# A vision tower with routed experts: the token step rearranged on all engines

## The chip, the cores and the metric

The kernel runs on one core of a Trainium2 chip. The metric is the device time of one execution in microseconds (us). A core has five engines that run side by side, each with its own queue that it works through in order, and that meet only at semaphores: TensorE (PE in the profile: matmuls and turnings, that is transposes), VectorE (DVE), ScalarE (ACT), GpSimd (POOL) and SyncE (SP), which issues transfers. DMA engines move the data. TensorE writes into eight banks of PSUM, from which DVE and ScalarE copy into SBUF.

## The reference, cut to what matters

128 images of 64x64x3 make 16 patches each, 2048 tokens of 768 values. All is float32.

```python
h = patches @ W.T + b                                  # 768 -> 192
q, k, v = split(layernorm(h) @ W_attn + b_attn)        # 12 heads of 16, rotary on q and k
h = h + causal_attention(q, k, v) @ W_proj + b_proj    # 16 tokens of an image among themselves
x = layernorm(h)                                       # (h - mean) / sqrt(var + eps)
t = x / sqrt(mean(x * x) + eps) * norm_scale           # rmsnorm
g = t @ gate_w.T + gate_b                              # 16 experts
top 4, weights = softmax of the four values
y = sum over the four: weight * (swiglu(t @ mlp1_w + mlp1_b) @ mlp2_w + mlp2_b)
out = h + x + y
```

The mean of x * x after a layernorm is var / (var + eps), so both roots follow from the same variance; the kernel before computes the second from the values.

## The kernel before, in words

There are two phases. In the **token phase** 16 tiles of 128 tokens (8 images) go through seven stages, and the queues of all engines are written out by hand (`unrolled(STAGES, TILES, step)`): in step n every engine does stage 0 of tile n, stage 1 of tile n - 1, up to stage 6 of tile n - 6, in an order of its own, which its `step` function gives. So there are 22 steps, of which 6 to 15 have all stages. Stage 0 is the embedding (L410) and the first norm (DVE, with its root on POOL); 1 the turning of the normed tile (`xnT`), the product to q and k (L432) and to v (L436), the rotary products; 2 the turnings of q and k (L416), `spread_keys` (ScalarE, six copies), the scores (L448), their maximum and, as the kernel was, the exponential `prob` (L680); 3 the sums and inverses (`prob_sum` L815, `prob_inverse_own` L824), `p_pair` on POOL (L1106), its turning on DVE (`turn_probs`), `spread_probs` (ScalarE, four copies), the values (L476), and their copy `yT`; 4 the projection (L455), the second norm with two roots and the residual `base`; 5 the turning of the token (`tT`), the gate, the four largest; 6 weights, rank of each token within its expert, row numbers `row_i` (L940), the bias of the experts (L466), and the **scatters**: POOL sends each tile's packet (192 values, 16 weights, a token number) to four rows of `routed_rows` by four indirect DMAs (L1093).

Semaphores tell of each result; a `wait` is a wait on one. Two buffers each of `packet` and `row_i` go round. SP meanwhile loads one expert's weights in every step (seven DMAs) and the next x.

Between the phases, DVE computes `fill_i` (L964) once the last tile is counted; SP, ScalarE and POOL write 8, 6 and 2 regions' padding rows (L310), and a table of 79 tiles is made. In the **expert phase** each of 79 tiles of 128 rows is loaded (L384), turned (L562), copied to `rT` by ScalarE (L617, the copy helper's line, in `r_step` L712), multiplied with its expert's weights (L580, L584), gated (L719), multiplied again (L592) and added to the output by an indirect DMA (L1149).

The order of three queues in a step, cut to what the change moves:

```python
# PE: embed(0), turn xn(1), turn q, k(2), project(4), rank(6), turn token(5), qk_product(1),
#     turn_weights(6), gate(5), scores(2), values(3), experts_bias(6), v_product(1)
# ACT: packet(6), xnT(1), qT(2), spread_keys(2), tT(5), spread_probs(3), combT(6), square(4),
#      yT(3), prob(2), top_e(5), v_sb(1)
# POOL: p_pair(3), root(0), root(4), four scatters(6), second root(4), residual(4)
```

Of the kernel before, what the change touches and what calls it, by code (L numbers as in the profile page):

```python
# [8 lines left out]
ALU = mybir.AluOpType  # L9
# [7 lines left out]
P = 128  # L17
# [13 lines left out]
EPS = 1e-5  # L31
LIMIT, ALPHA = 7.0, 1.702
# [14 lines left out]
STAGES = 7  # L47
R_STAGES = 3
# [48 lines left out]
def build(nc, x, consts, w_tok, b_tok, w_qkv, b_qkv, w_proj, nscale, w_gate, b_gate,  # L97
          w1, b1, w2, b2, out):
    routed = nc.dram_tensor("routed_rows", (SPARE + P, ROW), F32, kind="Internal").ap()
    with ExitStack() as ctx:  # L100
# [28 lines left out]
        nscale_bc = sb("nscale_bc", [P, DIM])  # L129
        power = sb("power", [P, 1])  # L130
# [27 lines left out]
        stats2, mv2, ve2, rstd2 = sb("stats2", [P, 6]), sb("mv2", [P, 2]), sb("ve2", [P, 1]), sb("rstd2", [P, 1])  # L158
        x2, x2sq = sb("x2", [P, DIM]), sb("x2sq", [P, DIM])
        ssq, msq, rms = sb("ssq", [P, 1]), sb("msq", [P, 1]), sb("rms", [P, 1])  # L160
        t_row = [sb(f"t_row{i}", [P, DIM]) for i in range(2)]
        packet = [sb(f"packet{i}", [P, ROW]) for i in range(2)]
        tT = sb("tT", [HALF + 1, 2, P])
        top_v, top_i, top_f = sb("top_v", [P, 8]), sb("top_i", [P, 8], U32), sb("top_f", [P, TOPK])
# [5 lines left out]
        comb = sb("comb", [P, EXPERTS])  # L170
# [4 lines left out]
        row_f = sb("row_f", [P, TOPK])  # L175
# [31 lines left out]
        ps_e, ps_cT = banks[0][:, 0:DIM], banks[0][0:EXPERTS, 256:256 + P]  # L207
        ps_qk = banks[1][:, 0:2 * DIM]

        def turned(b, a, rows=HALF):  # L210
# [5 lines left out]
        ps_qT, ps_b = turned(3, 0), banks[3][:, 256:256 + DIM]  # L216
        ps_kT, ps_g = turned(4, 0), banks[4][:, 256:256 + EXPERTS]
        ps_v, ps_p = banks[5][:, 0:DIM], banks[5][:, 256:256 + DIM]
        ps_xT, ps_tT = turned(6, 0), turned(6, 256)
        ps_s = banks[7][:, 0:HEADS * GROUP]  # L220
        ps_tab = banks[3][0:1, 0:3 * SLOTS]
        ps_b1 = banks[4][:, 0:2 * ICH * EXPERTS]
# [9 lines left out]
        b1_turned = sem("b1_turned")  # L232
# [6 lines left out]
                 "ve2_ready rstd2_ready x2_ready base_ready ssq_ready msq_ready rms_ready t_row_ready t_turned packed "  # L239
                 "tT_ready gated top_v_ready top_i_ready top_f_ready top_d_ready top_e_ready einv_ready top_w_ready "  # L240
                 "onehot_ready onehot_w_ready comb_ready weights_ready token_ready chosen_ready ranked comb_turned "
                 "combT_ready b2_done base_full place_ready onehot_r_ready row_f_ready row_i_ready "
                 "chosen_before_ready").split()
        s = {n: sem(n) for n in names}
        scattered = [sem("scattered0"), sem("scattered1")]
# [17 lines left out]
        def rows_out(t, buf):  # L263

            return (t - buf) * 8 * TOPK
# [50 lines left out]
        def _(sp):  # L316
# [58 lines left out]
            for buf in range(2):  # L375
                sp.wait_ge(scattered[buf], 16 * TOPK * TILES // 2)
# [831 lines left out]
```

## Time and profile before

| | us |
|---|---|
| median of 3 runs (545.75 to 549.13) | 546.63 |
| the profiled execution: its time | 546.29 |
| its span | 544.6 |
| TensorE busy | 454.4 (83%) |
| DVE busy | 304.7 (56%) |
| ScalarE busy | 310.6 (57%) |
| POOL busy | 254.6 (47%) |

The rows further down come from one profiled execution. Times are from the start of the span. "Busy" is the time in which an engine had an instruction of its own in work; waits and DMA-issuing are not in it, and the ends of matmuls are modelled. In a timeline a row says when an instruction (or several of a line, merged) started, how long it took, and in brackets how long the engine had been idle before it and whose signal ended that: "remote" is a releaser that the profile can't name, "issue" a stretch in which the engine waited for nothing that it shows.

### The profile page before, as it was taken

Reading aid. Unit: us, or ns where it says so; the run is one execution under the profiler, and the core shown is the slowest. Engines: PE = TensorE matmul, PEld = TensorE weight load, DVE = VectorE, ACT = ScalarE, POOL = GpSimd, SP = SyncE. Lnnn points to the kernel's source line nnn. Section 1 sums busy time; section 2 is a strip of 40 time slices with the busy share of each in tenths; the row PEclk is TensorE's granted clock in tenths of the full one; section 3 lists DMA queues with packets and bytes.
Section 4 is the critical chain, followed back from the end, with each engine's and each line's share of the span. In section 5 each row is a group of like instructions: output and inputs, shape, how many; then the busy total and the mean of one; then the engine's idle time right before and its main releaser. Section 6 shows DMA issues by size and latency. Waiting matters only on the chain.

```text
span 544.6 us, 14479 instructions
## 1 busy us (share of the span) xinstructions
PE 454.4 (83%) x3865; PEld 394.8 (72%) x3866; DVE 304.7 (56%) x964; ACT 310.6 (57%) x832; POOL 254.6 (47%) x303
## 2 busy tenths in 40 slices
PE   3888988878887765129999999999999999999960
PEld 2666776557665544028999999999999999999950
DVE  0367978887787656304555555555555555555530
ACT  1248656665667631036667666667666667666630
POOL 1114576667766557502444444444444444444332
PEclk9989989999898655559999999999999999999995
DMA  8955455554541112431334333333333333433221
GB/s 220 267 145 164 138 158 165 172 162 149 158 121 40 40 42 85 135 104 37 58 63 63 54 53 61 61 61 59 57 52 61 61 61 54 62 51 62 41 24 21
DMA packets 41901, 49.55 MB, mean 91 GB/s; under 512 B 6387, under 2 KB 33251, under 8 KB 41860
## 3 DMA queue, kind: packets, MB, share of 16 engines
q1 hardware_dynamic: 26452, 33.48, 22.7%
q0 software_dynamic: 14544, 14.94, 16.9%
q10 hardware_dynamic: 864, 0.65, 0.4%
q8 instruction: 18, 0.29, 0.2%
q14 instruction: 23, 0.19, 0.1%
HBM read 30.82 MB, written 18.23 MB: 90 GB/s over the span
## 4 chain that ended last, share of the span: by engine, by line
PE 48%; DMA 12%; DVE 11%; issue 10%; ACT 5%; POOL 4%; SPq 4%; another core or an unknown queue 4%; POOLq 1%; DVEq 0%; ACTq 0%
PE bank L580 16%; PE bank L592 11%; PE bank L584 10%; DMA out_rows<-x_sb,wtok_sb 6%; PE bank L562 4%; DMA out_rows<-x_sb,wproj_sb 3%; PE bank L410 2%; POOL routed_rows L1093 2%; ACT p_spread L617 2%; ACT k_spread L635 2%; DMA out_rows<-x_sb,pT 1%; SPq L309 1%; DMA x_sb<-patches 1%; SPq L310 1%
## 5 line engine op out<-in xcount | busy, mean ns | idle before, releaser
L1149 POOL DMA_INDIRECT out_rows<-x_sb,wtok_sb x50 | 78.6, 1573 | 130.2 <-DMA out_rows<-x_sb,wtok_sb 73.8
L580 PE MATMUL bank<-rT,w_now 128*128 128x128 f32 x948 | 120.1, 277 | 0.9 <-ACT rT L617 0.9
L580 PEld LDWEIGHTS bank<-rT,w_now 128*128 128x128 f32 x948 | 117.2, 193 | 1.7 <-ACT rT L617 1.7
L1038 DVE TENSOR_TENSOR v_sb<-bank,w_now 128x384 f32<-128x384 f32 x79 | 44.1, 558 | 117.2 <-PE bank L584 97.3
L617 ACT ACTIVATE w_now<-w_sb 128x1158 f32 x79 | 92.5, 1171 | 6.9 <-issue 1.7
L592 PE MATMUL bank<-w_sb,p_spread 128*128 x474 | 90.3, 327 | 1.1 <-DVE p_spread L1057 1.1
L617 ACT ACTIVATE rT<-bank 128x256 f32<-128x256 f32 x79 | 30.3, 383 | 89.8 <-PE bank L562 69.0
L592 PEld LDWEIGHTS bank<-w_sb,p_spread 128*128 128x128 f32 x474 | 75.2, 190 | 1.5 <-issue 1.4
L584 PE MATMUL bank<-rT,w_now 64*128 64x128 f32 x948 | 74.9, 291 | 0.0
L1093 POOL DMA_INDIRECT routed_rows<-packet,row_i x64 | 63.3, 989 | 24.2 <-issue 22.3
L719 ACT ACTIVATE k_spread<-bank,w_now 128x128 f32<-128x128 f32 x237 | 69.3, 370 | 1.9 <-PE bank L584 1.9
L584 PEld LDWEIGHTS bank<-rT,w_now 64*128 64x128 f32 x948 | 59.6, 189 | 9.6 <-issue 0.2
L1050 DVE TENSOR_SCALAR x_sb<-bank,row_w 128x192 f32<-128x192 f32 x79 | 33.0, 418 | 29.7 <-PE bank L592 28.5
L1149 POOL DMA_INDIRECT out_rows<-x_sb,wproj_sb x20 | 31.3, 1564 | 38.2 <-DMA out_rows<-x_sb,wproj_sb 20.7
L410 PE MATMUL bank<-wtok_sb,x_sb 128*128 128x192 f32 x192 | 40.2, 367 | 9.9 <-DMA wtok_sb<-w_tok 6.4
L410 PEld LDWEIGHTS bank<-wtok_sb,x_sb 128*128 128x128 f32 x192 | 37.8, 220 | 10.0 <-DMA wtok_sb<-w_tok 6.1
L1057 DVE SCALAR_TENSOR_TENSOR p_spread<-k_spread,v_sb 128x384 f32<-128x384 f32 x79 | 43.3, 549 | 0.8 <-ACT k_spread L719 0.8
L1043 DVE TENSOR_SCALAR v_sb<-v_sb 128x384 f32<-128x384 f32 x79 | 34.9, 442 | 2.7
L635 ACT ACTIVATE k_spread<-bank,cst 96x256 f32<-96x256 f32 x96 | 36.4, 481 | 0.0
L617 ACT ACTIVATE p_spread<-pT 32x384 f32<-32x384 f32 x64 | 33.1, 518 | 0.7
L562 PE MATMUL bank<-cst,wtok_sb 128*128 128x128 f32 x100 | 22.3, 306 | 13.4 <-DMA wtok_sb<-routed_rows 13.4
L617 ACT ACTIVATE yT<-bank 128x384 f32<-128x384 f32 x16 | 7.8, 490 | 41.2 <-remote 37.9
(150 smaller groups left out, 634.6 us busy)
## 6 DMA issues: line engine op xcount, KB each, us to landing
x_sb<-patches SPq DMA_DIRECT2D x16, 384.0 KB, 3.4
w_sb<-w SPq DMA_DIRECT2D x32, 192.0 KB
wtok_sb<-routed_rows SPq DMA_DIRECT2D x50, 106.0 KB
w_sb<-w SPq DMA_DIRECT2D x16, 288.0 KB
w_sb<-w SPq DMA_DIRECT2D x64, 48.0 KB
wproj_sb<-routed_rows SPq DMA_DIRECT2D x20, 106.0 KB
out_rows<-h SPq DMA_DIRECT2D x16, 96.0 KB
routed_rows<-packet,row_i POOLq DMA_INDIRECT x64
```

The lines of the kernel that those rows point to most:

```text
L410: last = mm(ps_e, x_sb[buf][:, c, :], wtok_sb[:, c, :], start=(c == 0), stop=(c == PCH - 1))
L562: last = turn(ps_rT[buf % 2][:, c, :], rows[buf][:, a:a + P], ident)
L580: mm(dst[:, c * P:(c + 1) * P], w[:, a:a + P], t[:, part, :], start=(c == 0), stop=False)
L584: last = mm(dst[:, c * P:(c + 1) * P], w[k:k + half, REST + c * P:REST + (c + 1) * P], t[k:k + half, 1 - part, :], start=False, stop=(c == ...
L592: last = mm(ps_yo[buf % 2], act_sb[buf % 2][:, c, :], w2_sb[:, bass.ds(expert, 1), c, :].rearrange("p a f -> p (a f)"), start=(c == 0), st ...
L617: return nc.scalar.activation(dst, src, ACT.Copy)
L635: last = nc.scalar.activation(k_spread[:, :, :, h], ps_kT.rearrange("p c (j i k) -> p c j i k", j=PAIRS, i=2), ACT.Copy, scale=const("head ...
L719: last = nc.scalar.activation(gate_act[b][:, a:a + P], ps_glu[b][:, a:a + P], ACT.Silu, bias=w1_now[b][:, GLU_B + c:GLU_B + c + 1], scale= ...
L1038: V.tensor_tensor(lin[b].rearrange("p (c t) -> p c t", c=ICH), ps_lin[b][:, 0:INNER].rearrange("p (c t) -> p c t", c=ICH), w1_now[b][:, LI ...
L1057: V.scalar_tensor_tensor(act_sb[b].rearrange("p c t -> p (c t)"), gate_act[b], SILU_LIMIT, lin[b], ALU.min, ALU.mult).then_inc(r["act_read ...
L1093: G.indirect_dma_start(out=routed, out_offset=bass.IndirectOffsetOnAxis(ap=row_i[buf][:, k:k + 1].bitcast(U32), axis=0), in_=packet[buf][: ...
L1149: G.indirect_dma_start(out=out, out_offset=bass.IndirectOffsetOnAxis(ap=rows[b][:, ID_AT:ID_AT + 1].bitcast(U32), axis=0), in_=y_out[b % N ...
```

## The change

It rearranges the token phase; the expert phase is as it was but for one copy.

- TensorE: the turnings of xn, q, k and the token come first in a step, then the q and k product, rank, the weights' turning, the projection, the embedding, gate, scores, bias, v product, and the values last.
- ScalarE: `prob` moves from the end of a tile's stage 2 to the start of its stage 3, `yT` from stage 3 to stage 4, the copy `v_sb` from the end of stage 1 to stage 2. The packet's copy and the square are gone; the residual (h1 scaled by `gain` plus `shift`) is new here.
- DVE: `norm2` writes the token straight into the packet, with the product of both roots as its scale. `norm3`, `top_float`, `fill_packet`'s copy of the weights and `place_whole` are gone; `gain` and `shift` are new; the order is another.
- POOL: one operation makes the two roots of a tile from its variance; the second root and the residual sum are gone. A tile's scatters are issued one step later, the first ahead of `p_pair`, two behind it, the fourth behind the roots; the last two tiles' are issued in the last step.
- The norm's gain no longer multiplies the token: at the start four small matmuls and three DVE operations turn it into a column and scale the gate's weights, and in the expert phase `rT` is scaled by it, in two ScalarE copies of 128 columns instead of one of 256.
- Four packets go round instead of two, and `ps_b`, `ps_g` and `ps_cT` change banks.

```diff
+T_EPS, T_SCALE = EPS * EPS / (1.0 + EPS), (1.0 + EPS) ** -0.5
+PACKETS = 4
+        ps_e, ps_b = banks[0][:, 0:DIM], banks[0][:, 256:256 + DIM]
+        ps_qT, ps_g = turned(3, 0), banks[3][:, 256:256 + EXPERTS]
+        ps_s, ps_cT = banks[7][:, 0:HEADS * GROUP], banks[7][0:EXPERTS, 384:384 + P]
...
         @block.tensor                      # step, new order
+                if tile(1) is not None:
+                    bank_free(("xnT_ready", seen(1, 1)), ("tT_ready", seen(5, 1)))
+                    turn_halves(tile(1), ps_xT, xn, "xn_ready", "xn_turned")
+                ...                        # q, k (2)
+                if tile(5) is not None:
+                    turn_halves(tile(5), ps_tT, packet[tile(5) % PACKETS], "t_row_ready", "t_turned")
+                ...                        # qk_product(1), rank(6), turn_weights(6), project(4), embed(0)
                 if isinstance(tile(0), int) and tile(0) == 0:
...
+                    for c in range(2):
+                        a = c * (DIM - P)
+                        mm(ps_ns[:, c:c + 1], ns_line[:, a:a + P], ident[0:1, 0:1], start=True, stop=True)
+                    for c in range(2):
+                        last = mm(ps_ns[0:HALF, 2 + c:3 + c], ns_line[:, c * HALF:(c + 1) * HALF], ident[0:1, 0:1],
+                                  start=True, stop=True)
+                    last.then_inc(ns_turned, 1)
+                    pe.wait_ge(setup_dve, 5)
+                ...                        # gate(5), scores(2), experts_bias(6), v_product(1)
+                if tile(3) is not None:
+                    bank_free(("yT_ready", seen(3, 1)), ("place_ready", seen(6)))
+                    values(tile(3), (n - 3) % 2)
...
         @block.scalar                      # step, new order
+                # prob(3), xnT(1), qT(2), v_sb(2), tT(5), yT(4), spread_keys(2), combT(6), spread_probs(3)
+                if tile(4) is not None:
+                    act.wait_ge(s["shift_ready"], t + 1)
+                    nc.scalar.activation(h0[:, t, :], h1[:], ACT.Identity, bias=shift[:], scale=gain[:]
+                                         ).then_inc(s["base_ready"], 1)
+                # top_e(5)
...
-                    copy(rT[b0 % 2][:], ps_rT[b0 % 2]).then_inc(r["rT_ready"], 1)
+                    for c in range(2):
+                        last = nc.scalar.activation(rT[b0 % 2][:, c, :], ps_rT[b0 % 2][:, c, :], ACT.Copy,
+                                                    scale=ns_row[:, c:c + 1])
+                    last.then_inc(r["rT_ready"], 1)
...
         @block.vector
+            V.tensor_scalar(ns_row[:], ps_ns[:, 0:2], T_SCALE, None, ALU.mult).then_inc(setup_dve, 1)
+            V.tensor_scalar(ns_gate[:], ps_ns[0:HALF, 2:4], T_SCALE, None, ALU.mult).then_inc(setup_dve, 1)
+            V.tensor_tensor(gate_w, gate_w, ns_gate[:].unsqueeze(2).to_broadcast([HALF, 2, EXPERTS]), ALU.mult
+                            ).then_inc(setup_dve, 1)
...
             def norm2(t):
+                packed = packet[t % PACKETS]
+                dve.wait_ge(s["roots_ready"], t + 1)
+                wait(dve, scattered[t % PACKETS], rows_out(t, t % PACKETS))
+                V.tensor_scalar(packed[:, 0:DIM], h1[:], mv2[:, 0:1], roots[:, 0:1], ALU.subtract, ALU.mult
+                                ).then_inc(s["t_row_ready"], 1)
+                V.tensor_scalar(gain[:], roots[:, 1:2], 1.0, None, ALU.add).then_inc(s["gain_ready"], 1)
+                V.scalar_tensor_tensor(shift[:], mv2[:, 0:1], -1.0, roots[:, 1:2], ALU.mult, ALU.mult
+                                       ).then_inc(s["shift_ready"], 1)
...
             def place_sum(t):
+                if t >= 2:
+                    dve.wait_ge(scattered[(t - 2) % PACKETS], rows_out(t + PACKETS - 2, (t - 2) % PACKETS))
+                    V.tensor_reduce(row_i[buf][:], onehot_r[:], AX_X, ALU.add).then_inc(s["row_i_ready"], 1)
...
+                # DVE's new order: mark_experts(6), choose_experts(6), prob_sum(3), top_weights(6),
+                #  prob_inverse(3), prob_inverse_own(3), weigh_experts(6), combine(6), note_token(6),
+                #  [fill_i], rope_products(1), turn_probs(3), attn_add(4), attn_stats(4), place_all(6),
+                #  attn_aggr(4), rope_add(1), place_chosen(6), place_sum(6), norm2(4), embed_add(0),
+                #  embed_stats(0), top_max(5), embed_aggr(0), top_index(5), score_first(2),
+                #  score_second(2), score_max(2), norm(0), score_minus_max(2), add_bias(6)
...
         @block.gpsimd
+            def attn_roots(t):
+                pool.wait_ge(s["mv2_ready"], t + 1)
+                alone(pool)
+                G.tensor_tensor(ve2[:], mv2[:, 1:2].to_broadcast([P, 2]), eps2[:], ALU.add).then_inc(s["ve2_ready"], 1)
+                pool.wait_ge(s["ve2_ready"], t + 1)
+                wait(pool, s["t_row_ready"], t)
+                wait(pool, s["shift_ready"], t)
+                G.tensor_tensor(roots[:], ve2[:], power2[:], ALU.pow).then_inc(s["roots_ready"], 1)
...
             def step(tile, seen, n):
+                late = n - STAGES
+                if 0 <= late < TILES - 1:
+                    scatter(late, 0, 1)
                 if tile(3) is not None:
                     normalise(tile(3))
+                if 0 <= late < TILES - 1:
+                    scatter(late, 1, 3)
+                if tile(4) is not None:
+                    attn_roots(tile(4))
                 if tile(0) is not None:
+                    embed_root(tile(0))
+                if 0 <= late < TILES - 1:
+                    scatter(late, 3, TOPK)
+                if tile(6) == TILES - 1:
+                    scatter(tile(6), 0, TOPK)
```

## Rows read from the trace of the kernel before

**Rows 1.** Busy time by stretch: stretch, length, then each engine's us and instructions, clock, DMA.
```profile
14.00:62.00 48.00, 41.86 (x313) 33.53 (x313) 30.79 (x99) 26.53 (x75) 13.74 (x31) 0.96 0.67 180
...
130.30:141.70 11.40, 9.38 (x84) 7.09 (x84) 9.19 (x40) 7.16 (x23) 8.08 (x14) 1.00 0.56 165
...
177.00:189.00 12.00, 8.03 (x74) 6.21 (x77) 8.59 (x37) 6.99 (x21) 7.10 (x11) 0.72 0.15 46
...
235.00:544.60 309.60, 284.12 (x2528) 263.50 (x2528) 148.82 (x316) 190.96 (x474) 123.89 (x79) 0.96 0.34 54
```

**Rows 2.** Timeline of one full step: start, us, engine, line, out<-in, idle before <- releaser.
```profile
132.18 1.07 POOL L1093 DMA_INDIRECT routed_rows<-packet,row_i  x1 [0.75 <-issue]
...
132.22 0.86 PE L476 MATMUL bank<-p_spread,v_sb 128*32 128x128 f32 x24 [0.58 <-ACT p_spread L617]
...
136.08 0.96 POOL L1093 DMA_INDIRECT routed_rows<-packet,row_i  x1 [0.30 <-issue]
...
136.41 0.49 ACT L617 ACTIVATE yT<-bank 128x384 f32<-128x384 f32 x1 [3.28 <-remote]
...
137.19 0.35 DVE L815 TENSOR_REDUCE rsum<-prob 128x12 f32<-128x192 f32 x1 [0.38 <-issue]
...
137.93 0.33 ACT L617 ACTIVATE v_sb<-bank 128x192 f32<-128x192 f32 x1 [0.59 <-remote]
...
142.56 0.17 DVE L940 CAST row_i<-row_f 128x4 int32<-128x4 f32 x1
...
143.55 1.07 POOL L1093 DMA_INDIRECT routed_rows<-packet,row_i  x1 [0.73 <-issue]
```

**Rows 3.** Timeline: a step before any scatter, the first scatters, and a late step.
```profile
55.87 0.49 ACT L617 ACTIVATE yT<-bank 128x384 f32<-128x384 f32 x1 [0.30 <-PE bank L476]
...
64.05 0.86 PE L476 MATMUL bank<-p_spread,v_sb 128*32 128x128 f32 x24 [0.58 <-ACT p_spread L617]
...
66.89 0.49 ACT L617 ACTIVATE yT<-bank 128x384 f32<-128x384 f32 x1 [2.01 <-remote]
...
205.87 0.64 PE L416 MATMUL bank<-cst,t_row 128*96 128x128 f32 x2
...
206.28 0.96 POOL L1093 DMA_INDIRECT routed_rows<-packet,row_i  x1 [0.30 <-issue]
...
206.55 0.38 ACT L617 ACTIVATE tT<-bank 96x256 f32<-96x256 f32 x1 [2.74 <-PE bank L416]
```

**Rows 4.** Groups by line, the token phase: count, busy us, mean ns, idle before.
```profile
L1093 POOL DMA_INDIRECT routed_rows<-packet,row_i x52 | 51.7, 994 | 20.7 <-issue 19.1 <-DVE row_i L940 1.0 <-ACT x2sq L672 0.6
...
L1106 POOL TENSOR_TENSOR p_pair<-prob,rinv_own 128x192 f32<-128x192 f32 x32 | 17.5, 567 | 19.3 <-DVE rinv_own L824 19.3
...
L1084 POOL TENSOR_TENSOR rstd<-ve,power 128x1 f32<-128x1 f32 x32 | 17.6, 551 | 2.7
...
L416 PE MATMUL bank<-cst,qk 128*96 128x128 f32 x64 | 10.1, 283 | 7.4 <-issue 3.8 <-DVE h L946 3.6
...
L862 DVE SCALAR_TENSOR_TENSOR t_row<-x,rms,nscale_bc 128x192 f32<-128x192 f32 x15 | 9.9, 661 | 1.1 <-POOL rms L1084 1.0
...
L824 DVE TENSOR_TENSOR rinv_own<-rinv,cst 128x24 f32<-128x24 f32 x16 | 2.9, 184 | 0.5
```

**Rows 5.** Timeline of the late steps and of what follows them.
```profile
171.31 0.34 DVE L815 TENSOR_REDUCE rsum<-prob 128x12 f32<-128x192 f32 x1
...
216.72 0.16 DVE L964 TENSOR_TENSOR fill_i<-bank,cst 1x16 int32<-1x16 f32 x1
...
239.04 0.35 SPq L384 DMA_DIRECT2D wtok_sb<-routed_rows  x1
```

**Rows 6.** Timeline of one tile of the expert phase.
```profile
300.38 0.38 ACT L617 ACTIVATE rT<-bank 128x256 f32<-128x256 f32 x1 [0.92 <-issue]
...
300.67 0.88 ACT L719 ACTIVATE k_spread<-bank,w_now 128x128 f32<-128x128 f32 x3
...
301.00 1.47 PEld L580 LDWEIGHTS bank<-rT,w_now 128*128 128x128 f32 x12
```

More of the change, by code:

```diff
@@ L157, in build @@
         h1 = sb("h1", [P, DIM])
[L158 to L162, printed above, removed]
+        stats2, mv2 = sb("stats2", [P, 6]), sb("mv2", [P, 2])
+        eps2, power2, ve2, roots = (sb(n, [P, 2]) for n in ("eps2", "power2", "ve2", "roots"))
+        gain, shift = sb("gain", [P, 1]), sb("shift", [P, 1])
+        packet = [sb(f"packet{i}", [P, ROW]) for i in range(PACKETS)]
         tT = sb("tT", [HALF + 1, 2, P])
-        top_v, top_i, top_f = sb("top_v", [P, 8]), sb("top_i", [P, 8], U32), sb("top_f", [P, TOPK])
+        top_v, top_i = sb("top_v", [P, 8]), sb("top_i", [P, 8], U32)
         top_d, top_e, top_w = sb("top_d", [P, TOPK]), sb("top_e", [P, TOPK]), sb("top_w", [P, TOPK])
@@ L649, in step @@
             def step(tile, seen, n):
-                if tile(6) is not None:
-                    t, buf = tile(6), (n - 6) % 2
-                    act.wait_ge(s["t_row_ready"], t + 1)
-                    wait(act, scattered[buf], rows_out(t, buf))
-                    copy(packet[buf][:, 0:DIM], t_row[buf][:]).then_inc(s["packed"], 1)
+                if tile(3) is not None:
+                    t = tile(3)
+                    act.wait_ge(s["sc2_ready"], t + 1)
+                    wait(act, s["p_pair_ready"], 2 * t)
+                    wait(act, s["rsum_ready"], t)
+                    nc.scalar.activation(prob[:], sc2[:], ACT.Exp).then_inc(s["prob_ready"], 1)
                 if tile(1) is not None:
@@ L838, in attn_add @@
                 wait(dve, s["base_ready"], t)
+                wait(dve, s["t_row_ready"], t)
                 V.tensor_tensor(h1[:], ps_p, h0_of(t), ALU.add).then_inc(s["h1_ready"], 1)
@@ L1096, in residual @@
-            def residual(t):
-                pool.wait_ge(s["x2_ready"], t + 1)
-                G.tensor_tensor(base[:, bass.ds(t, 1), :].rearrange("p a d -> p (a d)"), h1[:], x2[:], ALU.add
-                                ).then_inc(s["base_ready"], 1)
+                for k in range(k0, k1):
+                    G.indirect_dma_start(out=routed, out_offset=bass.IndirectOffsetOnAxis(
+                        ap=row_i[t % 2][:, k:k + 1].bitcast(U32), axis=0),
+                        in_=packet[buf][:], in_offset=None).then_inc(scattered[buf], 16)
```

238 lines of the change are left out of this document (89 added, 149 removed).

## The prediction

> **What bounds the kernel now.** I read the stretches first. In the token phase (to about 216 us) no engine is full: in one full step of 11.4 us TensorE is busy 9.38, DVE 9.19, GpSimd 8.08 and ScalarE 7.16 [rows 1]. The expert phase, 309.6 us, has TensorE busy for 284.1 of them [rows 1]; the change leaves its loop alone but for one ScalarE copy. So the question is what closes the loop of 11.4 us.
>
> The timeline of one full step answers it [rows 2]. POOL starts the four scatters of a tile at 132.18, and the fourth at 136.08. The attention values (L476) are issued at 132.22 and end by the record at 133.08, yet ScalarE's copy of them (`yT`) starts at 136.41, after 3.28 us of idleness that the trace gives to no known releaser; the copy of `v_sb` then waits in the same way until 137.93. `prob` stands behind `yT` in ScalarE's queue, so DVE's `rsum` comes at 137.19, DVE reaches `row_i` at 142.56, and only that lets the next scatters start, at 143.55. The loop: first to fourth scatter 3.90, to `yT` 0.33, to `rsum` 0.78, to `row_i` 5.37, to the next scatter 0.99; in all 11.37, which is the step.
>
> Is it the scatters that make TensorE's signal late? Three places speak for a link. In a step before any scatter, `yT` starts 0.30 after ScalarE became free, released by the values themselves [rows 3]. In the first step with scatters the values end at 64.91 and `yT` starts at 66.89, 1.98 later [rows 3]. And near the end the token's turning goes from 205.87 to 206.51 beside scatters (one until 205.98, the next from 206.28), and its copy starts at 206.55, at once [rows 3]. So I take it that the values, issued together with a scatter, are signalled late, with what TensorE ends behind them; other matmuls beside scatters are not. Why, the rows don't say. The Trainium skill (SBUF — State Buffer, "Who interferes with whom") says that TensorE's ports are shared with nobody and that a DMA never contends with a compute engine. By that rule no signal would be late because of a scatter; the trace differs by 3.28 us in each step, if my reading of it is right, and the rule's outcome is the first rival below.
>
> **The change, part by part.**
> DVE loses the gain product `t_row` (0.66 us, L862), and three casts or small copies (`top_float`, the weights' copy in `fill_packet`, `place_whole`); it gains `gain` and `shift`, two operations on one column. All five are small, and I price them as L824, 0.18 each [rows 4]. Net -1.2 + 0.4 = -0.8 per step: 9.2 becomes 8.4.
> ScalarE loses the packet's copy and the square with its read-out, and gains one scaled copy for the residual: about -0.5, off the path, since it is busy 7.16 of 11.4 [rows 1].
> POOL loses the second root, its preparation and the residual sum, about 0.55 + 0.2 + 0.6, and makes two roots at once at the price of one (L1084, 0.55; the column more I price at 0.03) [rows 4]. It keeps 4 scatters of 0.99 plus 0.3 between them, 5.2 in all, `p_pair` 1.13, and two groups of root and preparation of 0.9 each [rows 4]: 8.1 of work. It isn't the bound by its sum. But the attention root now stands behind three scatters on POOL, and DVE's `norm2`, with everything behind it, waits for that root.
> TensorE does the same work in another order, and the scatters no longer wait for the step's own `row_i`, nor `prob` for `yT`. That cuts the loop above. What replaces it is one of two loops.
>
> Loop A, if signals are punctual, goes over DVE and POOL. DVE's own work is 8.4. From `rinv_own` POOL does `p_pair` 1.1, two scatters 2.6 and the roots 1.0, 4.7 in all; DVE has some 12 operations meanwhile, about 3.6 of its 8.4, so it waits 1.1. Small waits for `prob` and for TensorE I put at 0.9. T = 8.4 + 1.1 + 0.9 = 10.4.
>
> Loop B, if the values are still signalled late. They are now last on TensorE; POOL's last scatter of a step follows the embedding's root and comes about when the values are issued, and the next step's first scatter follows it at once: a train of two. The turnings that open the next step stand behind the values, so their signal is held too, and `xnT`, hence the q and k product, waits for it. TensorE's work after the turnings is 9.4 - 1.2 = 8.2 (q and k turned: 10.1/16 = 0.63 [rows 4], the tokens' and embeddings' pairs about as much again); before it come the first turning 0.3, the hold h, a copy of 0.4 and 0.1 of signals; sequencer gaps 0.4. T = 9.4 + h. For h I take the shortest row, since this train is of two and not of four: 1.98 after the values' end [rows 3], of which 0.3 is the turning itself: h = 1.7, T = 11.1. The ends for h are 0 (nothing held; loop A decides then) and 3.28 - 0.3 = 3.0 (a train of four [rows 2]); with two scatters the train is over 2.3 after its start; with the 0.9 by which the `v_sb` copy came after the last scatter [rows 2] that is 3.2, less the values' 0.86 and the turning's 0.3: h = 2.1, T = 11.5.
>
> **The sum.** Start and ramp (steps 0 to 5, until about 58): the gain's four small matmuls and three DVE operations delay the first norm by 1 to 1.5; then embedding beside attention instead of after it shortens the steps of 9 to 10. TensorE is busy 41.86 of 48 there [rows 1], so 6 is all there is; I take -2 net, ends +2 and -5. Full steps: nine at 11.4 - 11.1 = 0.3, -2.7; ends -9 (T = 10.4) and +1 (T = 11.5). Late steps: from `rsum` at 171.31 to `fill_i` at 216.72 are 45.4 us [rows 5], with TensorE at a granted clock of 0.72 and all engines half idle [rows 1]. Cutting the old loop shortens the first two of 12 us to about 10.5, the others little: -4.5, ends -1 and -7. Tail: from `fill_i` to the first row loads at 239.04 it is SP that issues eight pads, and it is untouched; POOL's last eight scatters end before it. 0. Expert phase: the copy of the turned rows is split in two with a scale. It starts at 300.38 and ends at 300.76, the next weight load that needs it is at 301.00 [rows 6]: 0.24 of cover. As plain copies two halves cost some 0.1 more, covered: 0. If that cover is gone, each tenth of a us costs 7.9 us over 79 tiles.
> Sum: -2 - 2.7 - 4.5 = -9.2 against the profiled execution's 546.29, that is 537; its time is 0.3 under the median shown, so 538 against 546.63.
>
> **The rivals.**
> Punctual signals (the skill's rule above, and loop A): nothing in the new order meets the hold, or it isn't what I think. For it: the turning at 205.87 isn't held, and one train of two is shorter than any I have seen. Then -2 - 9 - 6.5 = -17.5: 529. Chance 0.25.
> The hold lasts to the end of the train and beyond, or POOL's root behind three scatters adds to it: T = 11.4 to 11.6 a step, and only ramp and late steps give something: 543 to 547. For it: the `v_sb` copy at 137.93 comes 0.89 after the fourth scatter's end [rows 2]. Chance 0.25, with the case that the new order does nothing at all.
> Slower: the split copy in the expert phase. A 128x128 activation with a per-partition operand takes part in a group of three in 0.88 [rows 6], 0.29 apiece; the two would take 0.6 and the matmul still just finds them. If the scaled form costs 0.4 each, they end at 301.2, 0.2 late in each of 79 tiles: +16, and 538 becomes 554. It decides once the pair takes over 0.62. Against it: only scale and shape differ from a copy that the trace shows. Chance 0.1.
>
> **The numbers.** The forecast (534 to 542) has 0.4, the rivals 0.25, 0.25 and 0.1. A measurement of this kernel tells about 1% (5.5 us) from no change. Faster by over 1% means under 541.2: most of the forecast (0.35) and all of the first rival, 0.6 with rounding; within 1%: 0.3; slower: 0.1. The range takes in 529 and the second rival, and its ends leave 2 in 10 out: 527 to 548.
>
> **What would show it.** Right: steps of 10.9 to 11.3 us in the full stretch; `xnT` starting 1.5 to 2 us after the record of its turning ends, again without a known releaser, while POOL runs two scatters in a row; DVE waiting at the rope products. The first rival: `xnT` starting at once, and DVE waiting instead at `norm2` for POOL's root, steps near 10.4. The slower rival: TensorE waiting for `rT` in every expert tile, and that phase over 310 us. The late stretch from the last embedding to `fill_i` should be 41 us, not 45. I am wrong if the held signal turns up in other places (the q and k product beside scatters two and three), or if POOL's order makes DVE wait for more than 1.5 us a step.

## The result, and the profile after

The changed kernel takes 556.8 us (median of 4 runs, 554.2 to 559.8) against 547.0 in the runs beside it: a ratio of 1.016, with a 95% interval of 1.012 to 1.021. It is slower by 9.8 us. Forecast were 538, a range of 527 to 548, and a chance of 0.1 for slower. The profiled execution took 555.65 us.

From the page of the changed kernel, whose span is 554.0 us: the granted clock of TensorE in 40 slices of 13.85 us, in tenths.

```profile
PEclk9999998888988955557999999999999999999995
```

TensorE is busy 458.8 us where it was busy 454.4, and of the seven slices from the seventh to the thirteenth, all in full steps, six have an 8 for the clock, where the kernel before had two. To see where the time went I cut the span where the prediction cut it, by DVE's `rsum` (one in each tile's stage 3; DVE's start times are the plainest clock of a step). Timeline of the kernel before, the fourth `rsum`:

```profile
57.66 0.34 DVE L815 TENSOR_REDUCE rsum<-prob 128x12 f32<-128x192 f32 x1
```

Timeline of the changed kernel: the first tile's embedding sum, the second tile's embedding, the fourth and the fourteenth `rsum`, and `fill_i`.

```profile
14.41 0.35 DVE L759 TENSOR_TENSOR h<-bank,btok_bc 128x192 f32<-128x192 f32 x1
...
20.91 2.59 PE L410 MATMUL bank<-wtok_sb,x_sb 128*128 128x192 f32 x12
...
60.41 0.35 DVE L822 TENSOR_REDUCE rsum<-prob 128x12 f32<-128x192 f32 x1
...
181.76 0.34 DVE L822 TENSOR_REDUCE rsum<-prob 128x12 f32<-128x192 f32 x1
...
222.12 0.15 DVE L962 TENSOR_TENSOR fill_i<-bank,cst 1x16 int32<-1x16 f32 x1
```

| stretch | before | after | forecast of the difference |
|---|---|---|---|
| start and ramp, to the fourth `rsum` | 57.66 | 60.41, +2.75 | -2 |
| ten full steps, to the fourteenth `rsum` (171.31 before [rows 5]) | 113.65 | 121.35, +7.7 | -2.7 (nine) |
| late steps, to `fill_i` (216.72 [rows 5]) | 45.41 | 40.36, -5.05 | -4.5 |
| tail, to the first expert product (242.20 before, 248.23 after) | 25.5 | 26.1, +0.6 | 0 |
| expert phase | 302.4 | 305.8, +3.4 | 0 |

The sum is +9.4, the difference of the two spans. The full steps hold most of it. A view by stretches (busy us and instructions of TensorE, its weight loads, DVE, ScalarE and POOL, then the granted clock) of three full steps of the changed kernel, and of the head of the second of them:

```profile
119.20:131.00 11.80, 8.95 (x84) 6.97 (x85) 8.43 (x38) 7.09 (x20) 6.81 (x11) 1.00 0.57 176
131.00:144.20 13.20, 10.58 (x84) 8.02 (x84) 8.52 (x38) 7.20 (x20) 6.49 (x11) 0.87 0.43 129
144.20:154.90 10.70, 9.28 (x83) 7.00 (x83) 8.49 (x38) 7.11 (x20) 7.13 (x11) 1.00 0.57 170
...
131.00:133.40 2.40, 0.81 (x6) 0.55 (x6) 1.96 (x12) 0.46 (x2) 2.07 (x4) 1.00 0.80 198
133.40:137.00 3.60, 3.22 (x11) 2.04 (x12) 0.66 (x2) 3.56 (x11) 2.23 (x3) 0.65 0.41 144
```

Each of the three steps has the same work (83 or 84 matmuls), but they last 11.8, 13.2 and 10.7 us. The longest has a mean clock of 0.87: in its first 2.4 us TensorE is busy 0.81, and in the 3.6 us behind that the mean clock is 0.65. Its timeline, and the end of the same step:

```profile
129.78 0.86 PE L476 MATMUL bank<-p_spread,v_sb 128*32 128x128 f32 x24
...
130.33 1.06 POOL L1080 DMA_INDIRECT routed_rows<-packet,row_i  x1 [0.26 <-issue]
...
130.98 0.39 PE L416 MATMUL bank<-cst,xn 128*96 128x128 f32 x2 [0.33 <-issue]
...
131.69 0.96 POOL L1080 DMA_INDIRECT routed_rows<-packet,row_i  x1 [0.30 <-issue]
...
133.30 0.38 ACT L622 ACTIVATE xnT<-bank 96x256 f32<-96x256 f32 x1 [1.81 <-remote]
...
133.75 0.17 PEld L416 LDWEIGHTS bank<-cst,packet 128*96 128x96 f32 x2 [2.20 <-issue]
...
136.36 1.91 PE L455 MATMUL bank<-wproj_sb,yT 128*128 128x192 f32 x6
...
143.00 0.86 PE L476 MATMUL bank<-p_spread,v_sb 128*32 128x128 f32 x24
...
143.86 1.13 POOL L1080 DMA_INDIRECT routed_rows<-packet,row_i  x1 [0.27 <-issue]
...
144.20 0.39 PE L416 MATMUL bank<-cst,xn 128*96 128x128 f32 x2 [0.34 <-issue]
...
144.63 0.38 ACT L622 ACTIVATE xnT<-bank 96x256 f32<-96x256 f32 x1
```

The values (L476) start at 129.78; a scatter starts at 130.33, while they run. The turning of xn (L416, 130.98) is over at 131.37, but ScalarE's copy `xnT` starts at 133.30, with 1.81 idle and no known releaser. That is the late signal that the prediction described. TensorE cannot go on, since its next turning waits for that copy: 2.20 us of idleness ahead of the weight load at 133.75. And what the prediction did not have: the clock falls to 1.2 GHz behind this idle head, and the projection (L455) takes 1.91 us at 136.36, against 1.14 in the steps at 2.4 GHz. At the end of the step the values start at 143.00 and the scatter at 143.86, just when they are over. There the copy of the turned xn starts at 144.63, 0.04 after the turning ends, and that step is the one of 10.7 us. The trace itself holds the experiment: same order, same scatters, no overlap with the values, and a punctual `xnT`.

The ends of matmuls are modelled, so the products themselves could have ended late and not only their signal. The trace also records when each semaphore was raised, and these records speak against it. The values' signal comes at 133.24, and those of the turnings of xn, q and k behind them at 133.28, 133.32 and 133.37: four signals in 0.13 us, for turnings that take 0.83 us by their rows. In the step of the kernel before [rows 2] the v product's signal comes at 137.90 and that of the embedding behind it at 138.03, although the embedding is 2.11 us of work. Timeline of the kernel before:

```profile
134.28 2.11 PE L410 MATMUL bank<-wtok_sb,x_sb 128*128 128x192 f32 x12
```

So TensorE had done this work before its signals were released, in order, in one burst. Where nothing is held a signal comes within 0.05 us of its product's recorded end.

Expert phase, the same view of the kernel before, its first 10 us:

```profile
242.20:252.20 10.00, 9.52 (x65) 8.47 (x66) 2.95 (x7) 5.09 (x14) 0.00 (x0) 0.75 0.27 69
```

The same of the changed kernel:

```profile
248.20:258.20 10.00, 9.26 (x52) 8.07 (x53) 1.55 (x4) 3.90 (x9) 0.00 (x0) 0.54 0.26 65
```

About half of the 3.4 us lies at the beginning, where the clock is 0.54 and not 0.75 for the first 10 us, and 52 matmuls are recorded instead of 65. The other half is spread over the tiles. Timeline of the kernel before, the gating of the 6th and of the 76th tile:

```profile
265.15 0.88 ACT L719 ACTIVATE k_spread<-bank,w_now 128x128 f32<-128x128 f32 x3
...
513.76 0.88 ACT L719 ACTIVATE k_spread<-bank,w_now 128x128 f32<-128x128 f32 x3
```

The same two tiles in the changed kernel:

```profile
273.29 0.88 ACT L719 ACTIVATE k_spread<-bank,w_now 128x128 f32<-128x128 f32 x3
...
523.65 0.88 ACT L719 ACTIVATE k_spread<-bank,w_now 128x128 f32<-128x128 f32 x3
```

70 tiles take 248.6 us before and 250.4 after, 0.025 us more a tile. The nine versions below that have the split copy take 250.3 to 250.9; e4, which has one copy as the kernel before, takes 248.6. The split copy is the only change in this phase, so I put these 1.7 us or so down to it; no run moved it alone. The whole phase took 303.3 to 306.0 us in the versions below.

### The profile page after: what moved, and what is told of

It reads as the page before. It is cut to its first block, busy times and chain, and to the rows that moved or that the text cites. A ratio compares the mean times of both kernels' runs of the same rounds, so it can differ in the third digit from the quotient of the medians.

```text
span 554.0 us, 14421 instructions
## 1 busy us (share of the span) xinstructions
PE 458.8 (83%) x3873; PEld 393.2 (71%) x3874; DVE 296.5 (54%) x935; ACT 327.9 (59%) x879; POOL 236.6 (43%) x260
## 4 chain that ended last, share of the span: by engine, by line
PE 57%; issue 12%; DMA 12%; DVE 8%; POOL 4%; SPq 3%; POOLq 1%; ACT 1%; DVEq 0%; ACTq 0%
PE bank L585 16%; PE bank L597 11%; PE bank L589 10%; DMA out_rows<-x_sb,wtok_sb 6%; PE bank L567 4%; PE bank L416 3%; DMA out_rows<-x_sb,wproj_sb 3%; PE bank L455 3%; PE bank L433 2%; PE bank L432 2%; PE bank L410 2%; POOL roots L1099 1%; SPq L309 1%; DMA wqkv_sb<-b_qkv 1%; DMA out_rows<-x_sb,pT 1%
## 5 line engine op out<-in xcount | busy, mean ns | idle before, releaser
L585 PE MATMUL bank<-rT,w_now 128*128 128x128 f32 x948 | 122.5, 280 | 1.4 <-ACT rT L710 1.4
L585 PEld LDWEIGHTS bank<-rT,w_now 128*128 128x128 f32 x948 | 114.2, 195 | 6.2 <-ACT rT L710 2.2
L710 ACT ACTIVATE rT<-bank,ns_row 128x128 f32<-128x128 f32 x158 | 49.3, 363 | 77.3 <-PE bank L567 62.0
L410 PE MATMUL bank<-wtok_sb,x_sb 128*128 128x192 f32 x192 | 37.2, 347 | 5.4 <-DMA wtok_sb<-w_tok 5.4
L410 PEld LDWEIGHTS bank<-wtok_sb,x_sb 128*128 128x128 f32 x192 | 35.3, 208 | 6.3 <-DMA wtok_sb<-w_tok 5.1
L622 ACT ACTIVATE xnT<-bank 96x256 f32<-96x256 f32 x16 | 6.1, 379 | 37.8 <-PE bank L416 23.9
```

The costliest lines, as they stand in the source:

```text
L410: last = mm(ps_e, x_sb[buf][:, c, :], wtok_sb[:, c, :], start=(c == 0), stop=(c == PCH - 1))
L585: mm(dst[:, c * P:(c + 1) * P], w[:, a:a + P], t[:, part, :], start=(c == 0), stop=False)
L622: return nc.scalar.activation(dst, src, ACT.Copy)
L710: last = nc.scalar.activation(rT[b0 % 2][:, c, :], ps_rT[b0 % 2][:, c, :], ACT.Copy, scale=ns_row[:, c:c + 1])
```

## The experiments

A late signal is priced at 1.9 us from here on, and a fall of the clock at 1.4; both come out of the runs. Times of before are those of the same chip.

### Only the place of the values: e1 and e11

```diff
# e1, TensorE's step
+    values(3)             # ahead of the experts' bias
     experts_bias(6)
     v_product(1)
-    values(3)
# e11, TensorE's step: only the last two exchanged
     experts_bias(6)
+    values(3)
     v_product(1)
-    values(3)
```

> The changed kernel with the values (L476) moved on TensorE from the end of the step to ahead of the experts' bias, so that they end about 1.5 us before POOL's last scatter of the step starts. Theory (hold and clock): values issued beside a scatter are signalled about 1.9 us late together with the turning behind them; TensorE then stands idle for 2 us at the head of the step, and its granted clock falls to 1.2 GHz behind that. Without the coincidence xnT starts within 0.3 us of its turning, no stretch of 0.5 granted clock stands in the full steps, a step takes 10.4 to 10.8 us instead of 12.6, and the whole about 537 us (533 to 541). Rival (the new order itself, with DVE waiting for POOL's roots, sets 12.6 us): 554 to 558. Rival (any matmul beside a scatter is signalled late): the turnings at the head are still beside two scatters, xnT is still 1.8 us late, about 556.

> The changed kernel with only the last two products of TensorE's step exchanged: the values (24 small matmuls of 32 columns) ahead of the v product (4 matmuls of 128x192), so that the v product and not the values is in work when POOL starts the fourth scatter, with the first of the next step right behind it. Nothing else is moved. Theory of the prediction (only the values are signalled late, with what stands behind them): xnT punctual, steps of 9.9 to 10.4, 533 to 541. Rival (whatever TensorE has in work when scatters start is signalled late, as the turnings were in the kernel before with the wait): xnT 1 to 2 us late, steps of 11.4 to 13, 548 to 558.

e1 took 536.9 us against 548.0 (ratio 0.980, 0.974 to 0.986), e11 537.8 against 552.3 (0.976, 0.969 to 0.983). Two neighbouring products exchanged on one engine are worth 19 us of 557 by the medians, 22 by the ratios to the kernel before on each chip. Timeline of e11 at the turn of a step:

```profile
132.28 0.86 PE L476 MATMUL bank<-p_spread,v_sb 128*32 128x128 f32 x24
...
133.99 1.13 POOL L1080 DMA_INDIRECT routed_rows<-packet,row_i  x1 [0.27 <-issue]
...
134.33 0.39 PE L416 MATMUL bank<-cst,xn 128*96 128x128 f32 x2 [0.34 <-DVE xn L774]
...
134.76 0.38 ACT L622 ACTIVATE xnT<-bank 96x256 f32<-96x256 f32 x1
```

The values are over at 133.14, before the scatter; the v product ends as the scatter starts, at 133.99. The turning at 134.33 runs beside the first scatter of a train of two, and `xnT` starts at 134.76, 0.04 after its end. In e1, ScalarE waited 0.0 us ahead of `xnT` in 11 steps, where the changed kernel had 12.5 in 10. So the late `xnT` comes from the overlap of the values with a scatter. That a turning beside a scatter is late as a rule, one of e1's rivals, falls.

One step of e1 by stretch:

```profile
100.30:111.70 11.40, 10.36 (x83) 7.80 (x83) 8.40 (x38) 7.11 (x20) 6.70 (x11) 0.85 0.53 153
```

Most steps take 9.9 to 10.1, less than the 10.4 that I had expected. Two took 11.3 or 11.4, one of them shown, with no late signal and a mean clock of 0.85: a fall of the clock alone costs 1.4. I had expected none; idle time of 1.07 to 1.26 ahead of xn's turning, here for DVE, is left at each head. e11, with 0.34 to 0.52 idle there, still has one such step, of 11.3.

Because the v product ended as the scatter started, e11 did not test what it was written for, whether other products are held. That took one more run.

### Other matmuls in work when the scatter starts: e12

```diff
# on top of e11, TensorE's step
     v_product(1)
+    wait qk_ready(1)
+    6 x turn(ps_kT, k)    # written again by the next step
```

> The version with values and v product exchanged, and 6 turnings of 128x96 (12 small matmuls, some 0.9 us, their result is written again by the next step's turning of k) at the very end of TensorE's step, so that full-width matmuls are in work when the fourth scatter starts, as the values were in the changed kernel. Rival (any matmul in work when a scatter starts is signalled late, with what follows): xnT 1 to 2 us late, steps of 11.5 to 13, 550 to 560. Theory (only the values' kind is held): xnT punctual; the added work costs 0 to 0.9 us a step, 9.9 to 10.8, so 537 to 547.

540.7 against 547.8 (0.983, 0.975 to 0.990). Timeline of e12:

```profile
135.86 0.82 PE L547 MATMUL bank<-cst,qk 128*96 128x128 f32 x6
...
136.02 1.13 POOL L1085 DMA_INDIRECT routed_rows<-packet,row_i  x1 [0.27 <-issue]
...
136.94 0.38 ACT L627 ACTIVATE xnT<-bank 96x256 f32<-96x256 f32 x1
...
137.41 0.40 PE L416 MATMUL bank<-cst,packet 128*96 128x128 f32 x2
...
137.45 0.96 POOL L1085 DMA_INDIRECT routed_rows<-packet,row_i  x1 [0.30 <-issue]
...
138.87 0.38 ACT L627 ACTIVATE tT<-bank 96x256 f32<-96x256 f32 x1 [1.07 <-PE bank L416]
```

The added turnings (L547, six matmuls by the trace) run until 136.68, and the scatter starts at 136.02 within them, as it did within the values. `xnT` is punctual (136.94; the turning ended at 136.90). So being in work when a scatter starts is not enough. But the turning of the token, issued 0.04 ahead of the next scatter, ends at 137.81 and its copy starts at 138.87, after 1.07 of idleness. Over 12 steps this wait adds up to 6.5 us (0.8 in e11), and the steps take 10.5 to 10.9. ScalarE waits 0.8 to 1.1 us in seven of the nine full steps and 0.25 in the other two, and by the semaphore records this turning's signal is 0.75 to 1.04 late in all nine. So a turning can be held too, by less, beside the second scatter of a train and with no values in work.

### The scatters moved instead of the values: e2, e7, e8

```diff
# e7, POOL's step
+    scatter(late, 3, TOPK)            # ahead of the embedding's root
     embed_root(0)
-    scatter(late, 3, TOPK)
# e2, on top of e7
+    wait(pool, s["pv_done"], ...)     # all values issued so far
     scatter(late, 0, 1)
# e8, on top of e2, behind embed_root
+    memset(junk[128 x 1100])
```

> The changed kernel, TensorE's order untouched; on POOL the fourth scatter goes ahead of the embedding's root and the next step's first scatter waits until the values of that step have ended. Theory (hold): the values meet no scatter, although the turnings behind them run beside the first one; steps of 10.4 to 11.0, about 539 us (534 to 544). Rival (any matmul beside a scatter is held): xnT still 1 us late or more, 548 to 556. Rival (order sets the step): 556 or more, as the embedding's root now stands behind one more scatter.

> The changed kernel with the fourth scatter ahead of the embedding's root on POOL, and no wait added: the next step's first scatter then starts right behind that root, where the fourth was, so the values meet one scatter that nothing follows for a microsecond, instead of two in a row. Theory (the late signal lasts to about 0.9 us after the last scatter of a train): xnT comes 0.5 to 1.0 us late instead of 1.9, TensorE's idle time at the head shrinks to about 1 us and the granted clock mostly stays, steps of 10.4 to 11, 537 to 544. Rival (a late signal has a fixed length whatever the train): 1.9 us late, steps of 11.8 to 13.2, 550 to 557. Rival (one scatter alone holds nothing): 9.9, 533 to 536.

> The kernel with both edits on POOL (fourth scatter early, first one behind the values), plus a memset of 128x1100 on POOL, about 1 us, in the place beside the values where the fourth scatter stood. Theory (the transfers that GpSimd issues delay the signal, not its work as such): no late signal, steps of 9.9 to 10.0, 533 to 537. Rival (any work of POOL beside the values delays them): xnT 1 us late or more, steps of 11 and above, 545 or more.

e2 took 534.7 against 548.0 (0.977, 0.971 to 0.983), with TensorE's order as in the changed kernel. One stretch of it:

```profile
101.00:111.00 10.00, 8.85 (x87) 6.97 (x83) 8.61 (x38) 7.00 (x20) 7.06 (x10) 1.00 0.55 176
```

Every full step takes 9.9 to 10.1 us at a clock of 1.00, and ScalarE waits 0.0 ahead of `xnT`. The hold has moved to where it costs nothing: the fourth scatter now starts while the scores (L448, also 32 columns wide) end, and by the semaphore records their signal is 0.4 us late in most steps, once 1.3.

e7, where the scores are held alike, took 540.4 against 548.8 (0.982, 0.974 to 0.990), within its range. Timeline of e7:

```profile
90.18 0.86 PE L476 MATMUL bank<-p_spread,v_sb 128*32 128x128 f32 x24
...
90.73 1.06 POOL L1080 DMA_INDIRECT routed_rows<-packet,row_i  x1 [0.24 <-issue]
...
91.38 0.40 PE L416 MATMUL bank<-cst,xn 128*96 128x128 f32 x2 [0.34 <-issue]
...
92.24 0.38 ACT L622 ACTIVATE xnT<-bank 96x256 f32<-96x256 f32 x1 [0.35 <-PE bank L416]
```

The values meet one scatter (90.73 to 91.79), with none behind it. `xnT` starts at 92.24, 0.46 after the turning's end and 0.45 after the end of the scatter. In the changed kernel it started 0.65 after the end of the second (131.69 + 0.96), and in the kernel before `v_sb` started 0.89 after the fourth [rows 2]. `yT` there came a little earlier, 0.33 after the fourth's start. So the hold grows with the train: the rival of a fixed length falls. Steps: 10.3 to 10.5, and two of 10.7 and 11.5 in which the clock fell (0.90 and 0.80).

e8 took 536.9 against 548.8 (0.980, 0.974 to 0.985). Its values beside the memset:

```profile
121.70 0.86 PE L477 MATMUL bank<-p_spread,v_sb 128*32 128x128 f32 x24
...
121.98 1.00 POOL L1127 MEMSET junk<- 128x1100 f32 x1
...
123.68 0.38 ACT L623 ACTIVATE xnT<-bank 96x256 f32<-96x256 f32 x1
```

The memset runs within the values, as the fourth scatter did, and `xnT` starts 0.03 after the turning: POOL's work as such holds nothing. The steps took 10.3 and not 9.9 to 10.0, since the memset stands ahead of the next scatter and of `p_pair` in POOL's queue; that I had left out.

### The clock: e5

```diff
# TensorE's step of the changed kernel, between the turnings of q and of k
+    12 x turn(ps_kT, k)
     turn_halves(k)
```

> The changed kernel with 12 more turnings of k on TensorE in each full step (the same result written again, some 1.8 us of work) between the turning of xn and that of k, where TensorE stood idle for 2 us at the head of the step. The late signal stays. Theory (the clock makes about half of the loss): the granted clock stays at 1.00 through the full steps, those of 13.2 us become 11.8, and the whole is 547 us (543 to 551). Rival (the clock has no part; the late signal and the order make the 12.6 us): no change, 555 to 558, or later by the work added where a step had no late signal. If the fall of the clock is set by something else than this idle time, the stretches of 0.5 stay and the time is 556 or more.

552.4 us (10 runs) against 548.0 (1.007, 1.004 to 1.010); the changed kernel had 556.8. ScalarE's copies of xnT between 60 and 180 us (count, busy us, mean ns, idle before):

```profile
L627 ACT ACTIVATE xnT<-bank 96x256 f32<-96x256 f32 x11 | 4.2, 380 | 14.7 <-remote 14.4 <-PE bank L416 0.4
```

A step of e5:

```profile
130.30:142.10 11.80, 10.20 (x103) 8.28 (x95) 8.37 (x38) 7.09 (x20) 6.67 (x10) 1.00 0.48 148
```

The late signal stays (14.4 us in 11 steps), but the clock is 1.00 throughout, and steps of 13.2 are gone: 11.7 to 12.0. That is 9.9 + 1.9. Filling idle time with useless turnings makes this kernel 4.4 us faster, so the clock has a part of its own. I had expected 9: the ten full steps became only 5.3 shorter (116.1), because steps without a late signal now pay for the filler (the first ones, of 9.9 and 10.4, became 11.0), and the ramp 1.6 longer, which the filler does not touch.

### The same cure for the kernel before: e4

```diff
# POOL's step of the kernel before
+    wait(pool, s["pv_done"], seen(3))   # this step's values
     scatter(6)                          # all four
```

> The kernel before with one wait more: POOL's four scatters start only when the step's values (L476) have ended. Theory (hold): yT starts 0.3 us after the values instead of 3.3; scatters start 0.9 us later, but row_i of the next step comes about 2.3 us earlier, and DVE or TensorE closes the step at 10.3 to 10.7 us instead of 11.4: about 537 us (533 to 542). Rival (the late signal has nothing to do with scatters): the wait delays the scatters and with them row_i, 11.4 to 12.3 a step, 547 to 556.

564.7 against 548.0: slower, 1.029 (1.022 to 1.035). Timeline of e4:

```profile
117.44 0.86 PE L476 MATMUL bank<-p_spread,v_sb 128*32 128x128 f32 x24 [0.77 <-ACT p_spread L617]
...
118.36 0.49 ACT L617 ACTIVATE yT<-bank 128x384 f32<-128x384 f32 x1
...
119.15 1.07 POOL L1093 DMA_INDIRECT routed_rows<-packet,row_i  x1 [2.39 <-PE bank L476]
...
123.05 0.96 POOL L1093 DMA_INDIRECT routed_rows<-packet,row_i  x1 [0.30 <-issue]
...
124.95 0.75 DVE L862 SCALAR_TENSOR_TENSOR t_row<-x,rms,nscale_bc 128x192 f32<-128x192 f32 x1 [3.12 <-POOL rms L1084]
...
124.97 2.27 ACT L635 ACTIVATE k_spread<-bank,cst 96x256 f32<-96x256 f32 x6 [1.07 <-remote]
...
125.44 1.09 POOL L1106 TENSOR_TENSOR p_pair<-prob,rinv_own 128x192 f32<-128x192 f32 x2
```

The late signal of the values is gone: `yT` starts at 118.36, 0.06 after the values' end, where it was 3.28 late [rows 2], and ScalarE waits 3.0 us for it in 9 steps, not 29.2 in 10. But the step became 12.4 to 13.7. The four scatters start at 119.15 and end at 124.01; in POOL's queue stand behind them the second root, the residual and the next `p_pair` (125.44). The root comes at 124.35, `t_row` on DVE at 124.95 after DVE has waited 3.12 for it, and `p_pair` leads over its turning and `spread_probs` to the next values at 129.84: a loop of 12.4 us that my wait had closed itself. I had counted the 0.9 us that the scatters start later, and not what is queued behind them. The clock fell more often as well: its mean over an execution is 0.87 to 0.89, against 0.91 to 0.93 in the kernel before on the same chip. e4 also shows turnings held beside a train of four with no values in it: `xnT` 0.9 late, and `k_spread`, whose turning ended at 122.28, starts at 124.97, again 0.96 after the last scatter (123.05 + 0.96). The theory "values only" is too narrow for long trains.

### The start, and the version that beats both: e9, e10

```diff
# on top of e2, in steps 0 to 5 (e9) or 0 to 3 (e10)
# PE:   embed(0) first in the step, not behind project(4)
# DVE:  embed_add, embed_stats, embed_aggr (0) first
# POOL: embed_root(0) first
# DVE:  the three operations on the norm's gain in step 1, not ahead of the first embed_add
```

> The kernel with both edits on POOL, and the start reordered: in steps 0 to 5 the embedding and its norm's sums go first on TensorE, DVE and POOL, as they did in the kernel before, and DVE's three operations on the norm's gain come after the first tile's sums. Theory (the change's start costs about 5 us against the old one: the sums of the fifth tile come at 72.4 us instead of 67.7): 3 to 5 us less than the kernel with both edits, 530 to 532. Rival (the ramp is bound by the attention chain, and the start is given back by the sixth step): 534 to 536. Rival (embedding first delays the turnings in these steps): 536 or more.

> The version with the reordered start, its old order (embedding first) kept only in steps 0 to 3 and the new one from step 4. In that version the steps 4 and 6 took 11.4 where the one with both edits on POOL took 9.5 to 9.9. If that is the price of embedding first once attention runs: 2 to 3.5 us less than 531.0, 527.5 to 529. Rival (the switch of orders itself costs a longer step, wherever it is): 530 to 532.

e9 took 531.0 against 548.8 (0.968, 0.962 to 0.973), 3.7 less than e2 beside a similar time of before. e10 took 528.9 against 552.3 (0.960, 0.953 to 0.966), as expected. It ran on another chip than e9, so the 2.1 us between them could be the chips', but between the second and third `rsum` it has 10.3 where e9 had 11.4, and between the fourth and fifth 10.1 where e9 had 11.6. In the second of these the clock of e9 fell (0.85 in the step from 57.8 to 69.2), so not all of it need be the price of embedding first. Its fourth `rsum` comes at 57.67, as in the kernel before (57.66). With the start as changed it came at 60.4 in the changed kernel, 62.3 in e2 and up to 64.2 (e12), so that start costs 3 to 6 us. e10 is 4% faster than the kernel before, and about 28 us faster than the change as made.

## Why the prediction was wrong

**The loop before: right as far as the rows go.** Scatters, late `yT`, `prob`, `rsum`, `row_i`, scatters. e4 removed the late signal by moving nothing but the scatters, and `yT` came at once. What the late signal costs in the old order is not shown, since e4 closed a longer loop. The other half of the reading, "other matmuls beside scatters are not", was wrong: the v product's signal (for `v_sb`, 137.93) came 1.5 us after the values' had been released, and e4 and e12 hold turnings.

**The late signal in the new order: right in place and size.** 1.7 was forecast, with a reach to 2.1; it is 1.8 to 1.9 in most steps. It sits where it was put, at `xnT`, behind the values and a train of two. The Trainium skill (SBUF — State Buffer, "Who interferes with whom") has a rule that a DMA never contends with a compute engine. I gave it 0.25 as a rival; e2, e7, e8 and e11 decide against what it would make of the time: they take the overlap away, all or in part, and gain 16 to 22 us. Whether a port has to do with it, no run shows.

**The step that failed: "T = 9.4 + h, T = 11.1".** Two terms of it. First, the base: it is 9.9 and not 9.4, so at full clock the held step is 11.8 (the one shown, and e5) and not 11.1. That alone turns the -2.7 into +4 for ten steps. The changed kernel's step from 119.18 to 130.98, at full clock, gives the terms: the turning 0.39, h 1.91, the copy and its signal 0.48, from the token's turning to the values' end 8.68, and 0.34 to the next turning. Timeline of the changed kernel, the token's turning in that step:

```profile
121.96 0.40 PE L416 MATMUL bank<-cst,packet 128*96 128x128 f32 x2 [1.96 <-issue]
```

The token's turning had been taken off the 9.4 with the other turnings, but it stands behind the hold, since it waits for `xnT`; that, the gaps between products (0.56 ahead of the experts' bias) and the first turning's own time are the missing 0.5. Second, a term that was not in the sum: the 2 us of idleness at the head of the step let the clock fall to 1.2 GHz in six of the nine steps, for another 1.4 each. 9.9 + 1.9 + 1.4 = 13.2. Seven of the ten steps of the table were held, which is 13 us over 9.9 a step, and the six falls are 8. I priced the hold as waiting only, although the clock was among the rows [rows 1]: 0.72 in the stretch where all engines are half idle. In the order before, the held signal cost TensorE less idleness, because it still had the bias and v product, the embedding and its turnings to do: 94.1 us busy of 113 in the full steps. In the new order the turning that is held opens the step, and everything of TensorE hangs on it. The Trainium skill (TensorE: Matmul & The Clock Gate, Part 1) says that the clock follows how busy TensorE has been of late; the trace agrees, since e5 kept it at 1.00 by work that nobody needs. The rule was there, and I did not weigh it.

**Loop A (punctual signals): right in kind, 0.5 too long.** 10.4 was forecast; 9.9 came, and 534.7 to 537.8 in all, where that rival had 529. The difference is the start (+4.7 in e2, where I had put -2) and the expert phase (+2).

**Start and ramp: wrong sign.** The first norm was to be 1 to 1.5 later, and the first embedding sum came 1.9 later (14.41, against 12.53 before). Not counted was that the second tile's embedding now stands behind the first tile's turning and q and k product: it starts at 20.91, before at 14.08. I had looked at TensorE's idle time in the ramp, and not at who the first tiles wait for.

**Late steps: right**, -5.05 for -4.5 (40.4 us for a forecast 41). **Tail:** +0.6 for 0. **The split copy:** 0 was forecast and about 1.7 us came, small beside the rival's 16. Timeline of the changed kernel, one pair:

```profile
304.96 0.63 ACT L710 ACTIVATE rT<-bank,ns_row 128x128 f32<-128x128 f32 x2 [0.82 <-PE bank L567]
```

The pair takes 0.63, where 0.6 was estimated and 0.62 was the point from which the slower rival decides; it ends at 305.59, and the weight load that needs it starts at 305.80, after 0.19 us in which the weight loads stood idle. The kernel is slower, then, but not by the mechanism that had the 0.1.

**Not settled:** why a signal of TensorE comes late beside GpSimd's indirect transfers, and what decides which product is held, and how long. The values (24 products of 32 columns) are held each time that a scatter starts beside them. The scores, 32 columns wide as well, are held by 0.4 us where the fourth scatter starts beside them. Turnings are punctual beside the first scatter of a train of two (e11, e12), held 0.8 us beside the second (e12), and 0.9 or more beside four. The runs bound the cause to the overlap with these transfers; whether the number of matmuls in flight, their shape or their place in the train decides, no run took apart.

## What to carry to other kernels

Ask of every wait not only how long it is but who is idle for it: in the order before, TensorE had other work while ScalarE waited three microseconds, and its clock fell in two full steps only; two microseconds at the head of TensorE's step cost 3.3, because the clock went down with them. When a signal comes late beside other work, first exchange neighbours in a queue so that the two don't overlap; a wait added for that purpose has to be followed through everything queued behind it (the same wait costs 17 us in e4, where four scatters stand behind it in a row, and gains about 6 from e7 to e2, where they are spread out; the steps of the profiles say the same, but the intervals of the two ratios overlap). And cut the start out of a pipelined kernel as a stage of its own: an order that is best for full steps cost 3 to 6 us in the first four.

## What the runs showed of the hardware

- TensorE's semaphore signals come late beside indirect transfers issued by GpSimd. The values' own signal is some 1.1 us late with one scatter (e7), 2.5 to 2.6 with two in a row (the changed kernel), 2.7 to 3.4 with four (full steps of the kernel before); the turning of xn right behind them is then 0.4 late with one and 1.7 to 1.9 with two. What waits for the last held signal starts 0.45 to 0.96 after the end of the last scatter. Held signals come out in order, 0.04 us apart. DVE's, ScalarE's and GpSimd's own signals in the token phase of the kernel before and the changed one are all recorded within 0.15 of their instruction's end, and a memset on GpSimd in the same place does not do it (e8).
- The granted clock fell to 1.2 GHz in six of the seven full steps that opened with 2 us of idleness, and in two of e1's, whose steps open with 1.07 to 1.26; each fall costs 1.4 us of a step that has 9 us of TensorE's work.
